# A four-layer decoder in one kernel: bias on GpSimd, causal mask with the maximum, loads moved between the quads

## The reference

```
x = _layernorm(x + _L0_attn_ref(x, ...))            # self attention with rotation, 16 heads of 8
x = _layernorm(x + _L0_xattn_ref(ctx, x, ...))      # cross attention, own layernorm
x = _layernorm(x + _L0_ffn_ref(x, ...))             # gated, 4 x 512 hidden
x = _layernorm(x + _L1_attn_ref(x, ...))            # state-space scan
x = _layernorm(x + _L1_xattn_ref(x, ctx, ctx, mask_BxSxS2, ...))
x = _layernorm(x + _L1_ffn_ref(x, ...))             # causal attention, 8 heads of 64, experts
x = _layernorm(x + _L2_attn_ref(x, ...))            # causal attention, 16 heads of 64, k = kv * (1 + w)
x = _layernorm(x + _L2_xattn_ref(x, ctx, ctx, ...))
x = _layernorm(x + _L2_ffn_ref(x, ...))             # convolution, routed experts
x = _layernorm(x + _L3_attn_ref(x, ...))            # self attention, shared projections
x = _layernorm(x + _L3_xattn_ref(x, ctx, ctx, mask_Bx1xSxS2, ...))
x = _layernorm(x + _L3_ffn_ref(x, ...))             # shared and 7 routed experts, top 2
```

## Time and profile before

| | us |
|---|---|
| median of 3 runs | 3258.83 (3252.49 to 3266.7) |
| the profiled execution | 3253.52 |
| its span | 3251.8 |
| PE busy | 2725.2 (84%) |
| DVE busy | 2036.4 (63%) |
| ACT busy | 1339.1 (41%) |
| POOL busy | 962.9 (30%) |

### The profile page before, as it was taken

How to read it: one execution, slowest core, us unless ns; L and a number is a source line. 1 busy time by engine, 2 the same in 40 slices (tenths; PEclk the granted TensorE clock), 3 DMA queues, 4 the chain that set the end, 5 groups by cost and what they waited for, 6 DMA issues and landing times. The chain is left out here.

```text
span 3251.8 us, 44820 instructions
## 1 busy us (share of the span) xinstructions
PE 2725.2 (84%) x16256; PEld 1271.1 (39%) x16256; DVE 2036.4 (63%) x4829; ACT 1339.1 (41%) x2299; POOL 962.9 (30%) x1206
## 2 busy tenths in 40 slices
PE   4998778978875988998988999968863999698997
PEld 1332334433322443454563444443431233254555
DVE  4884772159996755666784655656576876573444
ACT  1665553256552551221213433425641667263221
POOL 3111200048895101333342555552044110200000
PEclk9998789988877899999999999997875999698999
DMA  4220310000002300122230000003001220420000
GB/s 126 42 45 32 67 19 20 0 1 0 1 0 74 72 19 6 41 50 54 50 70 19 1 1 1 1 3 65 14 0 22 43 42 16 101 42 1 1 1 14
DMA packets 45655, 95.71 MB, mean 29 GB/s; under 512 B 14246, under 2 KB 33498, under 8 KB 39598
## 3 DMA queue, kind: packets, MB, share of 16 engines
q1 hardware_dynamic: 43708, 90.96, 12.8%
q10 hardware_dynamic: 1728, 1.89, 0.3%
HBM read 46.20 MB, written 1.38 MB: 15 GB/s over the span
## 5 line engine op out<-in xcount | busy, mean ns | idle before, releaser
L1819 POOL TENSOR_TENSOR mamba_dbu<-mamba_du,mamba_b 128x512 f32<-128x512 f32 x128 | 244.4, 1909 | 41.1 <-DVE stream L1849 12.3
L1849 DVE TENSOR_TENSOR_SCAN stream<-mamba_da,mamba_dbu 128x512 f32<-128x512 f32 x128 | 216.7, 1694 | 17.1 <-issue 11.9
L1579 PE MATMUL ps<-stream,weights 128*128 128x512 f32 x256 | 157.9, 727 | 58.8 <-DVE stream L1859 43.1
L559 DVE TENSOR_REDUCE L0a_negmax<-ps 128x1 f32<-128x512 f32 x256 | 162.4, 683 | 50.1 <-PE ps L302 49.7
L559 DVE TENSOR_REDUCE L3a_negmax<-ps 128x1 f32<-128x512 f32 x256 | 162.4, 683 | 49.8 <-PE ps L302 49.4
L2681 DVE TENSOR_REDUCE skv_negmax<-ps 128x2 f32<-128x1024 f32 (+3 forms) x128 | 101.1, 798 | 129.8 <-PE ps L2524 129.8
L405 ACT ACTIVATE L0a_probs<-ps 128x512 f32<-128x512 f32 x256 | 143.5, 599 | 76.3 <-PE ps L321 74.5
L405 ACT ACTIVATE L3a_probs<-ps 128x512 f32<-128x512 f32 x256 | 143.7, 600 | 74.1 <-PE ps L321 72.6
L2743 ACT ACTIVATE skv_probs<-ps 128x1024 f32<-128x1024 f32 (+3 forms) x128 | 90.1, 704 | 187.0 <-PE ps L2550 187.0
L164 POOL TENSOR_SCALAR vareps<-mv 128x4 f32<-128x4 f32 x24 | 9.8, 410 | 508.3 <-DVE mv L1319 508.1
L189 PE MATMUL ps<-stream,xT 128*64 128x512 f32 x512 | 129.3, 623 | 12.8 <-DVE moa_v L2306 6.6
(11 more groups left out here) (624 smaller groups left out, 6581.9 us busy)
## 6 DMA issues: line engine op xcount, KB each, us to landing
moa_masks<-picked SPq DMA_DIRECT2D x32, 512.0 KB
stream<-stream SPq DMA_DIRECT2D x28, 192.0 KB
stream<-gate_up_down_in SPq DMA_DIRECT2D x1, 4352.0 KB, 17.2
stream<-value_output_in SPq DMA_DIRECT2D x1, 4096.0 KB, 12.0
moa_gateb<-gates SPq DMA_DIRECT2D x32, 128.0 KB
stream<-ffn_in SPq DMA_DIRECT2D x1, 2888.0 KB, 9.9
L0a_qs<-L0a_qs SPq DMA_DIRECT2D x16, 128.0 KB
L0x_qs<-L0x_qs SPq DMA_DIRECT2D x16, 128.0 KB
```

Source lines behind the costliest of these rows:

```text
L559: dve.tensor_reduce(negmax[:, hh // G % 4, a, hh % G:hh % G + 1], ps[:, i % S_RING, :], AX.X, ALU.max, negate=True).then_inc(s["maxed"], 1)
L1579: pe.matmul(ps[:, SUM_BANK + j, :], k.ident, hc[:, (J * i + j) % RING, :], start=n == 0, stop=n == N - 1).then_inc(s["summed"], 1)
L1819: pool.tensor_tensor(dbu[:, m % RING, :], du[:, b % 2, j, :], bsb[:, i % B_RING, :], ALU.mult).then_inc(s["dbu_ready"], 1)
L1849: dve.tensor_tensor_scan(out=hs[:, m % RING, :], data0=da[:, m % RING, :], data1=dbu[:, m % RING, :], initial=0.0, op0=ALU.mult, op1=ALU.a ...
```

## The change

Eight things change. (1) The start loads only const and L0a's weights on SP, and the four xT and bconst on ACT; x, ctxT and the eight weight groups are issued by SP in L0a's loop, one step each from J = 0, and who reads them waits for `xT_in` or `x_in`. (2) GpSimd clears the buffers behind the first only when `first_parts` has reached 2. (3) `stack_q(1)` on SP waits for `turned_0`. (4) The streamed weights come in 16 pieces at J = 0 to 15 of the cross attention before. (5) The blocks of their own are gone; their loads and waits stand in the stages. (6) In the self attentions GpSimd adds x and the bias (`add_bias`), and DVE adds that instead of x. (7) The mask is no longer added by matmuls; DVE adds it (`later`, bf16) and takes the maximum in one fused instruction for each bank, writing the masked scores back to PSUM. (8) The last stage issues each batch's output when it is ready; the last turn of x is gone.

```diff
+PIECES = 16
-B_CONSTS = [("ident", P), ("halves", 2 * P), ("tri", 2 * P), ("sel", 2 * P),
+B_CONSTS = [("ident", P), ("later", SEQ), ("sel", 2 * P),
 # self attention, PE
-                        last = pe.matmul(at, out_t[:, t * P:(t + 1) * P], w(k, name, "wo"), start=True, stop=False)
-                        last = pe.matmul(at, w(k, "const", "one", 1), w(k, name, "bo", 1), start=False, stop=True)
+                        last = pe.matmul(at, out_t[:, t * P:(t + 1) * P], w(k, name, "wo"), start=True, stop=True)
 # GpSimd
+                def add_bias(b):
+                    if b == 0 and rotated:
+                        pool.wait_ge(k.x_in, 16 * BATCH)
+                    if b:
+                        pool.wait_ge(s["y_read"], b)
+                    pool.tensor_tensor(x_bias[:, :, :], k.xs[:, b], w(k, name, "bo").unsqueeze(1).to_broadcast([P, NT, D]),
+                                       ALU.add).then_inc(s["biased"], 1)
+                    pool.wait_ge(s["biased"], b + 1)
                 for J in range(FIRST, LAST):
+                    if batch_at(J, ZT_AT + 2) is not None:
+                        add_bias(batch_at(J, ZT_AT + 2))
...
                     if batch_at(J, SRC_AT + 2) == 0:
-                        for n in range(HALVES):
+                        clear(0)
+                        pool.wait_ge(s["first_parts"], 2)
+                        for n in range(1, HALVES):
                             clear(n)
 # DVE
                     dve.wait_ge(s["y_ready"], b + 1)
+                    dve.wait_ge(s["biased"], b + 1)
 # SP, self and cross attention
                 def stack_q(n):
                     b, buf = n // 2, n % HALVES
                     sp.wait_ge(*((s["first_parts"], 1) if b == 0 else (s["q_parts"], b)))
+                    if n == 1:
+                        sp.wait_ge(s["turned_0"], TURNED)
...
                 for J in range(FIRST, LAST):
+                    if 0 <= J < PIECES and load:
+                        load(sp, J)
                     if group_at(J, TURN_AT + 1) is not None:
                         put_maxima(group_at(J, TURN_AT + 1))
 # cross attention, GpSimd
                 for n in range(4):
+                    if n == 1:
+                        pool.wait_ge(s["first_parts"], 2)
 # expert and shared-key attention, PE
-                    for a in range(2):
-                        at = slice(WD * a, WD * a + WD)
-                        for c in range(2):
-                            last = pe.matmul(ps[:, S_BANK + a, qt * P:n], halves[at, c, :], tri[at, c, :], start=False, stop=True,
-                                             skip_group_check=True)
 # and DVE
-                    dve.tensor_reduce(negmax[:, g % 4, qt, at:at + 2], ps[:, S_BANK:S_BANK + 2, 0:(qt + 1) * P], AX.X,
-                                      ALU.max, negate=True).then_inc(s["maxed"], 1)
+                    n = (qt + 1) * P
+                    for a in range(2):
+                        last = dve.tensor_tensor_reduce(ps[:, S_BANK + a, 0:n], ps[:, S_BANK + a, 0:n], later[:, SEQ - n:], -1.0, 3e38,
+                                                        ALU.add, ALU.min, negmax[:, g % 4, qt, at + a:at + a + 1])
+                    last.then_inc(s["maxed"], 1)
 # routed_ffn
-                turn(BATCH - 1)
+            @block.sync
+            def _(sp):
+                for n in range(BATCH):
+                    sp.wait_ge(s["x_ready"], n + 1)
+                    sp.dma_start(out[n].rearrange("(t p) d -> p t d", p=P), k.xs[:, n]).then_inc(s["x_out"], 16)
+                sp.wait_ge(s["x_out"], 16 * BATCH)
 # build
+        def stream_in(src):
+            def piece(sp, n):
+                if n == 0:
+                    sp.sem_clear(stream_loaded)
+                a, z = (src.shape[1] * x // PIECES for x in (n, n + 1))
+                sp.dma_start(k.stream[:, a:z], src[:, a:z]).then_inc(stream_loaded, 16)
+            return piece
+        def load_rest(sp, n):
+            if n < BATCH:
+                sp.dma_start(k.xs[:, n], xin[n].rearrange("(t p) d -> p t d", p=P)).then_inc(k.x_in, 16)
+                sp.dma_start(k.ctxTs[:, n, :], ctxT[n]).then_inc(ctx_in, 16)
+            for g in [g for g in GROUPS if g not in ("const", "L0a", *LATER)][n - BATCH:][:1] if n >= BATCH else ():
+                load(sp, g)
 # start: SP loads const and L0a, and ACT:
+                for b in range(BATCH):
+                    act.dma_start(k.xTs[:, b, :], xTin[b]).then_inc(k.xT_in[b], 16)
+                    if b == 0:
+                        act.dma_start(k.bconst[:, :], bc[:, :]).then_inc(bloaded, 16)
+                act.wait_ge(bloaded, 16)
-        with nc.Block() as block:
-            @block.sync
-            def _(sp):
-                stream_in(sp, wstr0)
-        arrive(*(g for g in GROUPS if g not in ("const", "L0a", *LATER)))
-        cross_attention(k, "L0x", 1.0, scrambled=True)
-        depart("L2a")
-        gated_ffn(k, stream_loaded)
+        cross_attention(k, "L0x", 1.0, scrambled=True, load=stream_in(wstr0))
+        gated_ffn(k, stream_loaded, lambda sp: load(sp, "L2a"))
```

More of the change, by code:

```diff
@@ L2478, in shared_kv_attention, with _ @@
                    "sum_sb", "inverted", "normalized", "y_ready", "y_read", "xT_sb", *NORM_SEMS) as (block, s):
+            @block.sync
+            def _(sp):
+                load(sp)
             @block.tensor
@@ L2519, in scores @@
                         at, bank = slice(WD * a, WD * a + WD), S_BANK[i % 2] + a
[L2520 to L2525 removed]
+                        last = pe.matmul(ps[:, bank, 0:n], qT[at, r, qt * P:n], kT[at, r, 0:n], start=True, stop=True)
                     last.then_inc(s["scores"], 1)
@@ L3385, in load, with arrived, wait, rest_arrived @@
             sp.dma_start(k.weights[:, W_AT[g]:W_AT[g] + z - a], wres[:, a:z]).then_inc(loaded[g], 16)
-        def stream_in(sp, src):
-            sp.sem_clear(stream_loaded)
-            sp.dma_start(k.stream[:, 0:src.shape[1]], src[:, :]).then_inc(stream_loaded, 16)
+        def stream_in(src):
[11 more added lines that the diff above has]
+                load(sp, g)
+        def arrived(*groups):
+            def wait(sp):
+                for g in groups:
+                    sp.wait_ge(loaded[g], 16)
+            return wait
+        def rest_arrived(sp):
+            arrived(*(g for g in GROUPS if g not in ("const", "L0a", *LATER)))(sp)
+            sp.wait_ge(ctx_in, 16 * BATCH)
         with nc.Block() as block:
@@ L3423, in each @@
-        def each(stage):
-            for b in range(BATCH):
-                k.b, k.x, k.xT = b, k.xs[:, b], k.xTs[:, b, :]
-                stage(b)
-        R8 = DH ** -0.5
-        with nc.Block() as block:
-            @block.sync
-            def _(sp):
-                for g in GROUPS:
-                    if g not in ("const", "L0a", *LATER):
-                        load(sp, g)
-        self_attention(k, "L0a", R8)
-        with nc.Block() as block:
-            @block.sync
-            def _(sp):
-                stream_in(sp, wstr0)
@@ L3463, in build @@
-        cross_attention(k, "L3x", R8, biased=False, masks=(m3q, m3k, ALU.not_equal))
-        routed_ffn(k, stream_loaded)
-        with phase(k, "x_out") as (block, s):
-            @block.sync
-            def _(sp):
-                for b in range(BATCH):
-                    sp.dma_start(out[b].rearrange("(t p) d -> p t d", p=P), k.xs[:, b]).then_inc(s["x_out"], 16)
-                sp.wait_ge(s["x_out"], 16 * BATCH)
+        cross_attention(k, "L3x", R8, biased=False, masks=(m3q, m3k, ALU.not_equal), load=stream_in(wstr3))
@@ L3473, in block_diagonal @@
+        routed_ffn(k, stream_loaded, out)
 def block_diagonal(m):
@@ L3555, in bf16_consts @@
     r = np.arange(P)[:, None] % 64
[L3556 to L3558 removed]
+    put("later", np.concatenate([np.zeros((P, SEQ - P)), np.where(kk > q, MASKED, 0.0)], 1))
     put("sel", np.concatenate([np.broadcast_to(r // PARTS == c, (P, P)) for c in range(2)], 1))
```

107 lines of the change are left out of this document (48 added, 59 removed).

## The result

The changed kernel takes 3179.49 us (median of 4 runs, 3178.82 to 3180.67), the kernel before 3257.65 (4 runs); the ratio is 0.976 with a 95% interval of 0.9746 to 0.9773. Forecast were 3168 and a range of 3142 to 3200. Forecast against the profiled execution was a gain of 86.2.

What follows compares the result with a forecast made beforehand. PE was taken to bound the attention loops, and the cast and DMA chain the cross attentions' openings. Terms summing to 86.2 us off the profiled 3253.52 gave 3167.3; adding 0.7 made 3168, range 3142 to 3200.

Steps and rivals of the forecast that it cites:

- start: Kernel start: eight weight issues go, only 2.6 MB is waited for; first matmul at 8.65 us, gain 10.5 [8 to 12].
- self openings: First scores of both self attentions: faster casts, deferred second half, less load contention; gain 15.1 us [5.5 to 18].
- cross openings: Openings of four cross attentions: streamed loads gone, faster casts and turn; gain 17 us [8 to 27].
- bias: Self attentions' output bias off PE: 9.9 us in six loop batches, 4.3 at the ends; gain 14.2 us [4 to 16].
- mask: Causal attentions: 192 units lose four bf16 matmuls, DVE's two passes costed at nothing; gain 24.2 us, bounds 0 and 53.
- end: Kernel end: three output DMAs long gone, the last issued at once; gain 4.4 us [4 to 5].
- loads between quads: 48 weight pieces and the first stage's twelve loads share the ring with the maxima's rows; loss 4 us [0 to 12].
- rival A: Attention openings: the second half, waiting in `stack_q(1)`, is no earlier; about 22 us lost with piece losses, 3190; chance 0.15.
- Rival C: Masks cost 0.28 us a unit, cross openings give 27: 39 us more, 3129, half likelier, 3148; chance 0.12.
- Rival B: Mask gives nothing: DVE's two passes replace matmul time as latency, above all in expert attention; price 24 us, 3192; chance 0.13.
- Rival D: Fused pass on the same PSUM columns runs at half rate, 0.67 us more a mean unit: slower, 3321; chance 0.05.
- Rival E: Each of the 48 weight pieces puts 1.1 us on the path: 53 us lost, 3217; chance 0.05.

Runs made afterwards that it cites:

- the two mask versions: Changed kernel with the mask again as four bf16 matmuls per unit on PE, 3196.29 us; and with the mask left out of the maxima, 3175.78 us.
- A: The changed kernel itself, from which all experiments start; 3179.49 us, against 3257.65 us for the kernel before.

## Why the prediction was right

The direction and the range were right, and the mechanism was in every part but the cross attentions' openings. The sum was 13.4 us too large for the profiled execution (3167.3 against 3180.67). Some of the nearness is luck: three terms were too large by 22.5 us together, and the others too small by 9.6. By its terms, forecast and measured:

```
start                  10.5   10.5   first matmul 19.15 -> 8.63
self openings          15.1   11.3   first exponential 6.8 and 4.5 earlier in the stage
cross openings         17      6.7   first exponential: 0.7 later, 4.0 earlier, 1.0 later, 4.5 earlier
blocks                  4.8    4.9   PE's wait at ten boundaries between stages
bias                   14.2   18.6   L0a and L3a with the bias back on PE
mask                   24.2   15.8   L1g and L2a with the mask back on PE
end                     4.4    5.5   last stage, to the span's end
loads between quads    -4      0     L0x, L1x, L3x behind the first exponential: -0.3, +0.6, +0.1
sum                    86.2   73.3   span: 72.8
```

**Start.** 8.65 was taken, 8.63 measured. The mechanism was right; that it came out to 0.02 us is luck, for 8.65 was the middle of a range of 2.9 us, and its lower end was misread: by the earlier trace rows the 1.35 MB are reached at about 5.7 us, not 6.6. The blocks were right too: the boundary with two extra blocks fell from 2.52 to 1.31.

**Self attentions.** Right in kind. Putting the clearing back ahead made the first maxima 3.0 and 2.6 us later, near the 3.0 and 3.3 taken for the casts, but the stages only 1.7 and 2.0 longer. The deferred second half was worth 2.2 us at each first maxima and 3.6 in both stages instead of 6.2. The two together leave 2.4 us of L0a's 7.6 at the first maxima. They fit the 2.6 taken for the weight loads that moved away; no run took this apart.

**Cross attentions.** This is the step that failed. The forecast had "Between 1.0 and 4.4 I take 2 for each of four", and 17 for the stages; measured are 6.7. Two things were wrong. The 4.4 followed k's chain; the first scores now waited for q's, whose chain loses two slow casts where k's loses four. In L0x k's turn was issued 2.9 us earlier in the stage (11.0 against 13.8), q's 1.5 (10.4 against 12.0), and the first scores came only 1.7 us earlier (first maxima 18.1 us into the stage, before 19.8). And the second half was not 1.0 earlier but 1.2 later: it was issued at the first scores, and its way took 12.0 us (310.44 to 322.44), near the 12.5 I assumed, but it began 3 us later in the stage (17.7) than before (14.6). The forecast had the first scores 4.4 earlier, and since this did not come, the wait's price was not paid. That is rival A's mechanism at some 7 us instead of 22, and it is shown by the three versions without the wait: it accounts for about 7 of the 10.3 us that this term was short. Rival C, with 27 us from these openings and 53 from the mask, is refuted by both.

**Mask.** The mechanism was right, the size not. 192 units gave 0.08 us each instead of 0.126. Two things made the difference of 8.4. The matmuls alone were worth 20.5 us or 0.107 a unit (the two mask versions against each other), so the 0.11, read from one pair of records, was near, and the 0.27 for one unit in ten was not found; the 0.107 is a mean of 0.16 in the expert and 0.07 in the shared-key attention. The other 4 us are the fused passes in the expert attention, which I had put at nothing because DVE had room. It had room in the shared-key stretch, the one I had read; in the expert attention PE waits for DVE's other results, and these came later. Rival B expected a wait of the scores for each pass, because there is one pair of banks: that wait is 1.7 us in the whole stage, in two places, so B is refuted in its mechanism too. By the Trainium skill ("VectorE: DVE Perf Modes", section "The TRN2 errata — SBUF-src ops pay a fixed extra latency per instruction") the second pass would have cost 24 us, an estimate, if nothing hid it. The trace has more to hide: a pair of passes takes 0.18 to 0.21 us more than the one reduction did, some 37 us over 192 units, and about 4 of them were lost. Rival D needed 0.32 us a unit and is refuted: the second of the largest passes starts 0.61 to 0.62 us behind the first.

**Bias.** The term was mis-sized the other way. I counted half of the chain as gone (0.41 us a bias matmul). But the output matmuls, too, were slower beside them: inside the loops a batch fell from 3.29 us to 1.05, by 2.24 and not by 1.65. L0a's end fell from 4.2 us to 1.17 (284.45 to 285.62), not to 2.1; there the mean granted clock was 0.76 before and 1.00 after, so part of this is the clock.

**End.** 4.4 were taken. From the last x to the span's end it is 3.1 us, where it was 8.7.

**Loads between quads.** The cost of 4 was not found. Rival E did not happen with 16 pieces. The Trainium skill's rule ("DMA: Bandwidth & Descriptors", section "Queues, rings and completion order"), that one engine's DMAs are consumed in ring order, agrees with the trace of the single load, where the row behind it arrived some 10 us later: the row goes in packets of 1 KB, and none of that size starts between its issue at 326.75 and 335.86, while the load's packets run from 327.7 on. No run put rows and load on different engines' queues, so that the order, and not the traffic as such, held the row back is not shown. What is shown is that the size of the pieces keeps it off the path.

## What to carry to other kernels

In an opening where several transfers feed the first work, find the one that releases it: a gain on another chain is worth nothing, and a transfer held back until then starts its own 12 us from there. When a bulk load shares a queue with small urgent rows, cut it until one piece is hidden, and test the size: 16 pieces were free, 4 cost 11 us, 1 cost 39. A late row cost more than its wait here: the clock fell behind it. A one-row matmul for a bias cost more than its own time where it stood between others; add it elsewhere. Behind all of them it was cheaper, but in that version the output was no longer the reference's, so such an order needs its own way to keep the sums.

## What the runs showed of the hardware that I had not expected

Float32 matmuls of 128 columns went at 0.13 us a record in a row of eight (1.05 us for four of them), and at 0.21 when a matmul with a stationary operand of one row stood behind each (0.41 for each matmul, both kinds). With the same instructions sorted by kind the batch took 2.1 instead of 3.3 us. All this is at a granted clock of 1.00. What in the engine causes it no run here shows.

The granted clock fell to 0.50 behind three of six alternating batches, and around the one wait of 2.19 us for a late row, and stood there for 3.4 and 10.3 us. The last stage, the same code in all versions but the first kernel, took 281.5 to 281.8 us without a stretch at 0.50 inside it, 282.7 with one of 3.4 us and 285.0 to 285.3 with two. What decides these stays open. So does how much of the 5 us between the medians of A and of the version with the wait in the self attentions alone is its own.
